# Spreading the attention reciprocals by DMA instead of by matrix product in a one-core decoder layer

## The reference, cut to what matters

```
q, k, v = split(x @ Wqkv.T + bqkv)            # 16 heads of 32 channels
q, k    = elu(q * scale) + 1, elu(k * scale) + 1
denom   = max(sum over a head's channels of q * cumsum(k), 0.001)   # one per token and head
y       = q * cumsum(k * v) / denom
x = layernorm(x + y @ Wproj.T + bproj)
x = layernorm(x + channel_attention(x, ctx, ctx))   # 4 heads of 128 channels, global and local
x = layernorm(x + ffn(x))                     # 1 of 8 experts for each batch, 512 -> 2048 -> 512
```

## Time and profile before

| | us |
|---|---|
| median of 3 runs | 2344.71 (2343.95 to 2345.19) |
| the profiled execution, its own time | 2341.76 |
| its span in the trace | 2340.1 |
| PE busy / PEld busy | 2319.8 / 1917.2 |
| DVE busy / ACT busy / POOL busy | 1614.8 / 1133.2 / 377.2 |
| TensorE's granted clock, mean | 0.998 |

### The profile page before, as it was taken

How to read it: one execution, slowest core, us unless ns; L and a number is a source line. 1 busy time by engine, 2 the same in 40 slices (tenths; PEclk the granted TensorE clock), 3 DMA queues, 4 the chain that set the end, 5 groups by cost and what they waited for, 6 DMA issues and landing times.

```text
span 2340.1 us, 34103 instructions
## 1 busy us (share of the span) xinstructions
PE 2319.8 (99%) x12012; PEld 1917.2 (82%) x12012; DVE 1614.8 (69%) x2863; ACT 1133.2 (48%) x1878; POOL 377.2 (16%) x323
## 2 busy tenths in 40 slices
PE   9999999999999999999999999999999999999998
PEld 7878888888888888888888888888888888888787
DVE  8886685866768667586775867758677576865643
ACT  5344444454454544544455444544454444454553
POOL 1112211121111211202112021210112102121200
PEclk9999999999999999999999999999999999999999
DMA  9355445464554636546465464654547545463342
GB/s 343 92 153 189 117 144 163 140 219 114 153 163 128 228 107 185 137 131 225 113 184 140 143 196 131 193 131 149 173 130 211 122 144 177 134 166 98 103 116 89
DMA packets 113403, 361.10 MB, mean 154 GB/s; under 512 B 24914, under 2 KB 25042, under 8 KB 103122
## 3 DMA queue, kind: packets, MB, share of 16 engines
q1 hardware_dynamic: 80210, 319.02, 41.3%
q0 software_dynamic: 16896, 33.56, 9.0%
q10 hardware_dynamic: 16128, 6.34, 1.1%
HBM read 335.76 MB, written 23.12 MB: 153 GB/s over the span
## 4 chain that ended last, share of the span: by engine, by line
PE 96%; DVE 2%; ACT 1%; issue 1%; POOL 0%; DMA 0%; SPq 0%; POOLq 0%; DVEq 0%; ACTq 0%
PE acc L1329 29%; PE m L1103 13%; PE h_ps L1305 10%; PE h_ps L1307 10%; PE h_ps L1306 10%; PE m L1133 7%; PE m L1171 3%; PE m L1173 2%; PE m L1172 2%; PE m L1187 2%; PE m L1265 2%; PE m L1286 1%; PE acc L1103 1%; PE m L1144 1%; PE m L1157 1%
## 5 line engine op out<-in xcount | busy, mean ns | idle before, releaser
L582 ACT ACTIVATE hid<-h_ps,b 128x512 f32<-128x512 f32 x252 | 173.6, 689 | 597.2 <-PE h_ps L1307 596.5
L1103 PE MATMUL m<-xT_hi,wq 128*128 128x512 f32 x1320 | 408.0, 390 | 0.7 <-DVE xT_lo L1064 0.6
L1305 PE MATMUL h_ps<-x2T_hi,we_hi 128*128 128x512 f32 x1008 | 400.5, 397 | 2.3 <-DVE x2T_lo L953 2.3
L1329 PE MATMUL acc<-we_hi,h_hi 128*128 128x512 f32 x1008 | 400.8, 398 | 1.5 <-DVE h_lo L969 1.5
L1307 PE MATMUL h_ps<-x2T_hi,we_lo 128*128 128x512 f32 x1008 | 392.9, 390 | 0.0
L1329 PE MATMUL acc<-we_hi,h_lo 128*128 128x512 f32 x1008 | 392.8, 390 | 0.0
L1329 PE MATMUL acc<-we_lo,h_hi 128*128 128x512 f32 x1008 | 392.6, 390 | 0.0
L1306 PE MATMUL h_ps<-x2T_lo,we_hi 128*128 128x512 f32 x1008 | 392.5, 389 | 0.0
L969 DVE TENSOR_TENSOR h_lo<-hid,h_hi 128x512 fp32r<-128x512 f32 x252 | 203.5, 807 | 251.4 <-ACT h_hi L589 251.4
L959 DVE TENSOR_TENSOR we_lo<-raw,we_hi 128x1024 fp32r<-128x1024 f32 x256 | 329.6, 1288 | 30.9 <-ACT we_hi L572 30.9
L520 ACT ACTIVATE e_f<-m,sb_qkv,scale 128x512 f32<-128x512 f32 x116 | 90.5, 780 | 480.1 <-PE m L1133 477.9
(11 more groups left out here) (260 smaller groups left out, 3274.0 us busy)
## 6 DMA issues: line engine op xcount, KB each, us to landing
raw<-in_w SPq DMA_DIRECT2D x256, 512.0 KB, 4.4
wq<-wq_scratch SPq DMA_DIRECT2D x168, 512.0 KB, 3.8
x<-in_x_tok SPq DMA_DIRECT2D x16, 1024.0 KB, 6.6
x<-in_b_proj POOLq DMA_DIRECT2D x16, 1024.0 KB, 14.4
ctx_T<-in_ctxT SPq DMA_DIRECT2D x16, 1024.0 KB, 9.3
x<-in_b POOLq DMA_DIRECT2D x16, 1024.0 KB, 11.4
ctx_tok<-in_ctx_tok SPq DMA_DIRECT2D x15, 1024.0 KB, 4.7
out_dram<-x SPq DMA_DIRECT2D x15, 1024.0 KB, 5.0
```

Of the source, the lines that this page charges most:

```text
L582: act.activation(hid[:, f % 2, :], up_bank(b, f)[:, :], ACT.Relu, bias=b1[:, b % 2, f:f + 1]).then_inc(h_done, 1)
L1103: pe.matmul(bank(a, j)[:, :], w[:, s, t, :], x_hi[:, t, :], start=(t == 0 and s == 0), stop=False)
L1305: pe.matmul(ps, we_hi[:, g % NW, js], x2T_hi[:, j, :], start=(j == 0), stop=False)
L1329: last = pe.matmul(acc[t][:, :], hx[:, f % 2, ts], wx[:, g % NW, C:], start=(f == 0 and n == 0), stop=(f == FC - 1 and n == 2))
```

## The change

In batches 2 to 14 (`SPREAD_BY_DMA`) TensorE no longer spreads the reciprocals. SyncE stores `rden` to a DRAM scratch in one transfer (half step 20, behind the load of x); ScalarE waits for that store at the end of half step 21 and issues four loads, one for each chunk of 128 channels, that read 4 rows of 512 reciprocals, each repeated over 32 partitions, into `xT_lo`, which is free then. To make one load's partitions regular, the channels of the first block are put in another order on the host (`order`): within a chunk, partition `4 d + l` is channel `d` of head `l`. The mask `head_sum` is built to match. VectorE multiplies by what lies in `xT_lo` (chunks 0 and 1 at the end of half step 22, 2 and 3 in 23), and leaves out the rounded copy and the remainder. High and low parts, projection, column sums, split of x, first norm, Gram product and scores move half a step later (`LOW` two: 23 to 25), for batches 3 to 14; batch 2 had them there already but for Gram, scores and what follows `CTX_SUM`. `LOAD_CSUM` stays. Batches 0, 1 and 15 do as before.

```diff
+SPREAD_BY_DMA = range(2, NB - 1)
...
-SPREAD = plan(21, 20, 21, 22)
-HIGH = plan(22, 20, 21, 23)
-LOW = plan(23, 21, 23, 25)
-PROJECT = plan(25, 23, 25, 26)
-CTX_SUM = plan(26, 25, 26, 27)
-SPLIT_X = plan(29, 28, -6, 30)
-NORM_1 = plan(31, 29, 30, 32)
-GRAM = plan(33)
-SCORES = plan(34, 33)
+SPREAD = plan(22, 20, 21)          # each with its old value for batch 15
+HIGH = plan(23, 20, 21)
+LOW = plan(25, 21, 23)
+PROJECT = plan(26, 23, 25)
+CTX_SUM = plan(27, 25, 26)
+SPLIT_X = plan(30, 28, -6)
+NORM_1 = plan(32, 29, 30)
+GRAM = plan(34, 33, 33)
+SCORES = plan(35, 33, 34)
-KEEP_CSUM = plan(28)
+KEEP_CSUM = plan(29)
...
+        def spread_rows(a, cc):
+            return rden_dram[a, XH * cc:XH * cc + XH, :].unsqueeze(0).broadcast_to([HD, XH, T])
...
+                    if (a := at(i, h, DEN + 1)) is not None and a in SPREAD_BY_DMA:      # SyncE
+                        sp.wait_ge(rden_done, reciprocals_before(a) + 1)
+                        sp.dma_start(rden_dram[a].rearrange("r (s n) -> s r n", s=TT), rden[:, :]).then_inc(rden_st, 16)
...
-                if (a := at(i, h, RALL)) is not None:
-                    act.wait_ge(rden_done, 3 * a + 3)
+                if (a := at(i, h, RALL)) is not None and a not in SPREAD_BY_DMA:
+                    act.wait_ge(rden_done, reciprocals_before(a) + 3)
...
+                    if (a := at(i, h, RALL + 1)) is not None and a in SPREAD_BY_DMA:     # ScalarE
+                        act.wait_ge(rden_st, 16 * (a - SPREAD_BY_DMA.start + 1))
+                        for n in range(2):
+                            for cc in range(2 * n, 2 * n + 2):
+                                act.dma_start(y_lo(a)[:, cc, :].bitcast(F32),
+                                              spread_rows(a, cc)).then_inc(rden_in[n], 16)
...
             def times_reciprocal(a, cc):
-                dve.wait_ge(rb_mm, CC * a + cc + 1)
+                if a not in SPREAD_BY_DMA:
+                    dve.wait_ge(rb_mm, CC * spread_before(a) + cc + 1)
+                else:
+                    dve.wait_ge(rden_in[cc // 2], 32 * (a - SPREAD_BY_DMA.start + 1))
                 dve.wait_ge(num_done, CC * a + cc + 1)
-                dve.tensor_tensor(numer(a)[:, cc, :], numer(a)[:, cc, :], AB[(cc + 1) % 2][:, :], ALU.mult).then_inc(y_done, 1)
+                rb = AB[(cc + 1) % 2][:, :] if a not in SPREAD_BY_DMA else y_lo(a)[:, cc, :].bitcast(F32)
+                dve.tensor_tensor(numer(a)[:, cc, :], numer(a)[:, cc, :], rb, ALU.mult).then_inc(y_done, 1)
...
+                    if (a := at(i, h, SPREAD)) is not None and a in SPREAD_BY_DMA:       # VectorE, end of the half step
+                        times_reciprocal(a, 0)
+                        times_reciprocal(a, 1)
...
                 for n in range(2):
-                    if (a := at(i, h, SPREAD + n)) is not None:
+                    if (a := at(i, h, SPREAD + n)) is not None and a not in SPREAD_BY_DMA:   # TensorE
                         spread_reciprocal(a, 2 * n)
                         spread_reciprocal(a, 2 * n + 1)
...
+    order = np.arange(C).reshape(CC, XH, HD).transpose(0, 2, 1).reshape(-1)
+    wq, wk, wv = (w[order] for w in np.split(g["L0_attn_Wqkv"], 3, axis=0))
```

More of the change, by code:

```diff
@@ L53, in rank, with spread_before, reciprocals_before @@
     return min(b, BY_DMA.start)
+def spread_before(b):
+    return min(b, SPREAD_BY_DMA.start)
+def reciprocals_before(b):
+    return 2 * spread_before(b) + b
 def plan(usual, *first):
@@ L79 @@
 RALL = plan(20, 18)
-SPREAD = plan(21, 20, 21, 22)
-HIGH = plan(22, 20, 21, 23)
-LOW = plan(23, 21, 23, 25)
-PROJECT = plan(25, 23, 25, 26)
-CTX_SUM = plan(26, 25, 26, 27)
-SPLIT_X = plan(29, 28, -6, 30)
-NORM_1 = plan(31, 29, 30, 32)
-GRAM = plan(33)
-SCORES = plan(34, 33)
+SPREAD = plan(22, 20, 21)
+SPREAD[NB - 1] = 21
+HIGH = plan(23, 20, 21)
+HIGH[NB - 1] = 22
+LOW = plan(25, 21, 23)
+LOW[NB - 1] = 23
+PROJECT = plan(26, 23, 25)
+PROJECT[NB - 1] = 25
+CTX_SUM = plan(27, 25, 26)
+CTX_SUM[NB - 1] = 26
+SPLIT_X = plan(30, 28, -6)
+SPLIT_X[NB - 1] = 29
+NORM_1 = plan(32, 29, 30)
+NORM_1[NB - 1] = 31
+GRAM = plan(34, 33, 33)
+GRAM[NB - 1] = 33
+SCORES = plan(35, 33, 34)
+SCORES[NB - 1] = 34
 CTX_ROW = plan(35, 33, 36)
-KEEP_CSUM = plan(28)
+KEEP_CSUM = plan(29)
+KEEP_CSUM[NB - 1] = 28
 LOAD_CSUM = plan(31)
@@ L111, in build @@
     wq_dram = nc.dram_tensor("wq_scratch", [JOBS, P, 2 * CC * P], F32, kind="Internal").ap()
+    rden_dram = nc.dram_tensor("rden_scratch", [NB, SEG, T], F32, kind="Internal").ap()
     csum_dram = nc.dram_tensor("csum_scratch", [NB, C], F32, kind="Internal").ap()
@@ L184, in build @@
         small_in, consts_in = sem("small_in"), sem("consts_in")
+        fourth_done = sem("fourth_done")
+        rden_st, rden_in = sem("rden_st"), [sem("rden_in0"), sem("rden_in1")]
         rq_in = [sem(f"rq_in{j}") for j in range(JOBS)]
@@ L282, in build @@
         block = ctx.enter_context(nc.Block())
-        MADE = 11
+        MADE = 13
         head_ps = H_PS[:, :].rearrange("p (t c) -> p t c", t=CC)
@@ L400, in _ @@
                                    channel_multiplier=step_p).then_inc(made, 1)
+            pool.wait_ge(fourth_done, 1)
+            for cc in range(CC):
+                pool.tensor_copy(head_sum[:, cc, :].rearrange("p (r h) -> p r h", r=2)[:, :, XH * cc:XH * cc + XH],
+                                 fourth[:, :].unsqueeze(1).broadcast_to([P, 2, XH])).then_inc(made, 1)
             pool.wait_ge(made, MADE)
@@ L658, in mix @@
                     normalise(1, c)
-                if (a := at(i, h, RALL)) is not None:
-                    act.wait_ge(rden_done, 3 * a + 3)
-                    if (due := upto(a - 1, CC, CC)) is not None:
-                        act.wait_ge(rb_mm, due)
+                if (a := at(i, h, RALL)) is not None and a not in SPREAD_BY_DMA:
+                    act.wait_ge(rden_done, reciprocals_before(a) + 3)
+                    if spread_before(a) > 0:
+                        act.wait_ge(rb_mm, CC * spread_before(a))
                     for s in range(TT):
@@ L774, in denominator @@
                 dve.wait_ge(den_mm, a + 1)
-                if (due := upto(a - 1, TT, TT)) is not None:
-                    dve.wait_ge(rall_done, due)
+                if 0 < a <= SPREAD_BY_DMA.start:
+                    dve.wait_ge(rall_done, TT * a)
+                elif a > SPREAD_BY_DMA.start:
+                    dve.wait_ge(rden_st, 16 * (a - SPREAD_BY_DMA.start))
                 dve.tensor_scalar(den[:, :].bitcast(F32), den_ps, EPS_DEN, None, ALU.max).then_inc(den_max, 1)
@@ L1032, in mix @@
                 for n in range(2):
-                    if (a := at(i, h, SPREAD + n)) is not None:
+                    if (a := at(i, h, SPREAD + n)) is not None and (n == 1 or a not in SPREAD_BY_DMA):
                         times_reciprocal(a, 2 * n)
@@ L1060, in mix @@
                         split_x2(c, j)
+            dve.wait_ge(made, 7)
+            dve.reduce_sum(fourth[:, :], ident[:, :].rearrange("p (d l) -> p l d", l=XH), AX.X).then_inc(fourth_done, 1)
             for t in range(CC):
@@ L1161, in project @@
                     pe.wait_ge(wplo_done, 1)
-                if t < 2:
+                if t < 2 and a not in SPREAD_BY_DMA:
                     pe.wait_ge(y_done, CC * a + 3 + t)
-                else:
+                elif t >= 2:
                     pe.wait_ge(res1_done, TT * a + t - 1)
@@ L1446 @@
                            for w in (wk, wv, wq)], axis=1).reshape(JOBS, P, CC * P),
-        "w_proj": weights(g["L0_attn_Wproj"]).reshape(P, CC * C),
-        "b_qkv": column(g["L0_attn_bqkv"]),
+        "w_proj": weights(g["L0_attn_Wproj"][:, order]).reshape(P, CC * C),
+        "b_qkv": column(g["L0_attn_bqkv"].reshape(3, C)[:, order]),
         "scale": g["L0_attn_scale"].reshape(1, 1),
```

17 lines of the change are left out of this document (7 added, 10 removed).

## The result

The changed kernel takes 2375.01 us (median of 4 runs, 2373.32 to 2378.01), the kernel before, run beside it, 2344.33 (2343.72 to 2345.19): the ratio is 1.0131, with a 95% interval of 1.0118 to 1.0144, so **30.7 us slower** where +14.4 was forecast. The profiled execution has a span of 2374.0 us (own time 2375.9), 33.9 more than before.

The account below looks back on a forecast made before the run. TensorE, busy 99% of the span, was taken as the bound. Saving -11.8, round trip +20.8 and column sums +5.4 gave +14.4 on 2341.76, or 2356.2; with 2.95 for the runs' median, 2359 us, range 2335 to 2382.

Parts of the forecast that it names:

- The saving: TensorE without the `spread_reciprocal` matmuls gets back 0.91 us a batch in 13 batches, 11.8 us in all.
- The round trip: Store, four loads and VectorE's work in series make `h_lo` late for `down` of half step 25: +20.8 us.
- late by 1.6 us: `h_lo` ready at 1101.0 but due at 1099.4 for `down` of half step 25, in each of 13 batches.
- The middle, 1.4: On SyncE's queue the reciprocals' store lands 0.3 to 2.8 us after the x load; 1.4 us was taken.
- The last goes out 1.0 us later: After the store, ScalarE issues the four loads at 0.33 us each, the last 1.0 us later.
- just not late: ScalarE, held until about 1094.7, still has its ReLU done for `up` of half step 24 at 1096.7.
- The column sums: ScalarE, held by its wait for their later store, delays the x2 splits and TensorE's next projection job: +5.4 us.
- 0.45 us late: TensorE's projection job behind the x2 splits starts at 1132.4 against 1131.95, in 12 batches.
- under half: Sign in the profile: ScalarE idle 1.6 us ahead of the x2 splits, 12 times, TensorE losing under half of it.
- Both in time: Rival: store close behind the x load, loads landing in 5.1 us, last before 1097.3; 2333 to 2338 us, chance 0.20.
- The store is slow: Rival: 4 of 16 DMA engines carry the store, landing 2.7 us behind the x load; 2376 us, chance 0.17.
- Everything collides: Rival: loads as slow as 7.6 us and a late column sum together; 2390 us and more, chance 0.08.

Follow-up runs that it names:

- the best version: Changed kernel with column sums' store at half step 28, x load at 26, VectorE's second pair of multiplies behind `h_lo`: 2332.15 us, 0.9950 of the kernel before.

## Why the prediction was wrong in its size

**The saving was right.** 0.91 us a batch: 143.84 - 142.91 wherever no load is late, and 12.1 us in the best version against 11.8 forecast.

**The round trip: right mechanism, 25.5 us for 20.8.** The step "late by 1.6 us" held nearly: 1.81 in batch 8, and `h_lo` done 16.7 us after the reciprocal as forecast. Its pieces were off in opposite directions. "The middle, 1.4" behind the x load was wrong: in batches 5 to 14 the store is there 0.3 us before it, so the queue did not finish in order as the prediction had read from the weights' landing. The x load itself lands about 1 us later than it did (10.8 in the median against 9.8). "The last goes out 1.0 us later" was 1.9, since an issue of this 3-dimensional source takes 0.6 us. From first issue to last landing it took 6.4 us in place of 5.7. In the mean of batches 3 to 14 the last load landed at 15.0 where 14.7 was forecast. That the pieces came out so near is luck in part. ScalarE's "just not late" held in all batches but one: in batch 3 its ReLU came 1.17 us late.

**The column sums: the step that failed, 12.6 us for 5.4.** Of what lies between +14.4 and +30.7 this term is the largest part, 7.2 us, ahead of the round trip's 4.7 and the clock's 4.6. The chain was named rightly and ScalarE's hold was near (21.7 us in 12 times, 1.8 each; forecast 1.56). "0.45 us late" was that hold less a slack of 1.1 us, the difference of two larger numbers, and both were off. The hold was reckoned with the median landing of 9.7 us; past the point where the slack is gone every tenth counts in full, so the mean counts, and it was 10.1 with landings up to 11.4. And the slack was 0.75 (in batch 8 a hold of 2.89, TensorE late by 2.13): the step looked at the job alone and left out the fourth transpose ahead of it, which waits for the first bank, after which the job waits again for the second. 1.8 - 0.75 = 1.05 us, 12 times. That TensorE would lose "under half" of the hold was wrong: it lost more than half.

**The clock: left out, 4.6 us.** The sum priced an idle TensorE at the length of its gap. Three of twelve batches added 3.4 us of lower clock after it, 1.5 to 1.6 us each. With gaps of 2.1 to 2.8 us (`LOAD_XT` 23) it was ten of twelve; in the best version, which has no gap of 1 us or more in those batches, none. The means and what waits for the scores, both put at 0, cost 0.8 us once each; the moves alone show the same two kinds of wait.

**The rivals.** "Both in time" did not happen, but its price (2333) is what the best version measures once the two waits are gone. "The store is slow" gives 2376, almost the measured time, and is refuted all the same: it needs the store 2.7 us behind the x load, the first load goes out 2.0 us behind it at the most and in ten of thirteen batches at most 0.3, and the rest of the time comes from the column sums and the clock. The number alone would have borne out the wrong mechanism. "Everything collides" is nearest in kind for the loads: the runs that only gave the store or the x load another place in the same stretch kept most last landings at 14 to 16 us. It is not the whole: the last landing falls to 11.4 to 12.9 us in only half of the batches when the x load is far away.

**What stays open**: why two loads of 512 KB land later than four of 256; and what makes some last loads take 6 us and others 4 in the version with the x load far away. Its trace gives a hint that no run tests: last loads issued by 7.3 us after the reciprocal land at 11.4 to 13.5, those issued later at 12.7 to 15.4, and the next 512 KB of expert weights go out at 8.1 to 8.9. How much of the round trip is the store's is open too: even first in the queue, or without the x load, it holds the loads back for some 5 to 7 us from batch 3 on, and no run gives it the other shape there. That `KEEP_CSUM` at 29 costs 7, 12 and 17 us in three surroundings (the moves alone, the changed kernel, the x load at 26) follows the landings of its store, 9.67, 10.13 and 10.46 us in the mean: 12 times their differences is 5.5 and 4.0 us, and ScalarE is held 16.1, 21.7 and 25.6 us in all. Why they land later is open.

## What to carry to other kernels

When a round trip through DRAM replaces a product, look first at what stands behind its consumer on an in-order engine: here two multiplies moved behind an urgent operation were worth 20.6 us in the changed kernel, where the best change of the transfers, the x load far away, was worth 14.5. When a slot is shifted, move or keep both ends of every store-and-load pair; price the wait at the mean and the spread of the landing, not at its median, once the slack is gone. A gap on TensorE costs more than its length when the clock falls after it, as it did here behind gaps of about 2 us.

## What was unexpected of the hardware

- An issue of a load whose source repeats 4 rows over 32 partitions took 0.52 to 0.90 us (0.6 in the median) on ScalarE's queue, the 4-block store 0.60 on SyncE's; the same store in 128 rows and most plain loads take 0.33.
- A 64 KB store in 4 blocks behind a 1 MB load on the same queue was done some 0.3 us before that load in the mean of ten batches, and 2 us after it in two; in 128 rows, mostly 0.2 us after it.
- Two broadcasts of 512 KB landed later (14.8 to 16.9 us) than four of 256 KB (14.4 to 16.5).
- TensorE's granted clock fell to 0.5 for 3.4 us in 3 of 12 batches with gaps of 1.4 to 2.5 us, and in 10 of 12 with gaps of 2.1 to 2.8. One batch with a gap of 2.45 us had none.
